# A graph layer's node stage: six slots of x for four, and GpSimd loads two of the six

## What is computed

```python
h = relu(layernorm(x))
msg = relu(h[src] + edge_attr)
p = msg @ W_fc.T + b_fc                         # one row of 256 for each edge
w = exp(p @ Q.T - segment_max(p @ Q.T, dst)[dst])       # four heads
alpha = w / max(segment_sum(w, dst)[dst], 1e-9)
pooled[:, h] = segment_sum(alpha[:, h] * p, dst)        # for each head
gate = softmax((segment_sum(p, dst) / max(deg, 1)) @ Wg.T + bg)
out = x + sigmoid(sum_h gate[:, h] * pooled[:, h])      # one row of 256 for each node
```

## Time and profile before

| | |
|---|---|
| median of three executions | 657.8 us (657.22 to 658.36) |
| the profiled execution | 653.4 us, span of the profile 651.3 us |
| granted TensorE clock, mean | 0.968 |
| busy share of the span: TensorE, VectorE, ScalarE, GpSimd | 83%, 71%, 64%, 70% |
| DMA | 171.54 MB, mean 263 GB/s |
| chain that ended last, largest lines | TensorE L803 22%, TensorE L895 22%, L788 5%, ScalarE L649 4%, GpSimd L516 4% |
| first sigmoid of the node stage | at 327.94 us |

### The profile page before, as it was taken

How to read it: one execution, slowest core, us unless ns; L and a number is a source line. 1 busy time by engine, 2 the same in 40 slices (tenths; PEclk the granted TensorE clock), 3 DMA queues, 4 the chain that set the end, 5 groups by cost and what they waited for, 6 DMA issues and landing times.

```text
span 651.3 us, 12707 instructions
## 1 busy us (share of the span) xinstructions
PE 543.0 (83%) x2670; PEld 439.9 (68%) x2671; DVE 462.0 (71%) x1607; ACT 416.3 (64%) x765; POOL 454.9 (70%) x342
## 2 busy tenths in 40 slices
PE   2799999999999999920899989878878876878775
PEld 2588888888887778810687768666666665656554
DVE  3986878998999998779776667555646555456454
ACT  1667778888897888723035556656665665666674
POOL 6777777777777777107045677787887878778784
PEclk9998999999999999975799999999999999899999
DMA  8566666766668899530289999999999999999999
GB/s 206 165 198 166 201 194 211 219 203 204 197 189 284 295 300 315 181 129 1 72 285 350 386 345 320 320 331 351 312 318 326 354 314 334 318 304 348 327 342 324
DMA packets 137275, 171.54 MB, mean 263 GB/s; under 512 B 10132, under 2 KB 123820, under 8 KB 137238
## 3 DMA queue, kind: packets, MB, share of 16 engines
q10 hardware_dynamic: 91344, 90.23, 42.3%
q1 hardware_dynamic: 33046, 42.70, 20.6%
q0 software_dynamic: 12848, 38.20, 18.5%
HBM read 111.50 MB, written 59.60 MB: 263 GB/s over the span
## 4 chain that ended last, share of the span: by engine, by line
PE 54%; DVE 15%; ACT 9%; issue 8%; POOL 4%; ACTq 3%; DVEq 3%; DMA 3%; POOLq 0%; SPq 0%
PE bank L803 22%; PE bank L895 22%; PE bank L788 5%; ACT arena L649 4%; POOL arena L516 4%; DVE spread L1406 4%; ACT bank L625 3%; PE bank L800 3%; DVE stats L1214 2%; ACTq L652 2%; DVEq L1410 1%; DMA p_keep<-in_x_dram,idx 1%; DVE arena L1220 1%; DVEq L1406 1%; DMA arena<-in_x_dram 1%
## 5 line engine op out<-in xcount | busy, mean ns | idle before, releaser
L895 PE MATMUL bank<-p_keep,spread 128*128 x1172 | 274.5, 388 | 54.3 <-DVE spread L1406 43.4
L895 PEld LDWEIGHTS bank<-p_keep,spread 128*128 128x128 f32 x1172 | 218.7, 192 | 110.9 <-issue 83.7
L1406 DVE TENSOR_SCALAR spread<-bank,rel,wgt 128x128 f32<-128x128 f32 x586 | 195.6, 403 | 131.4 <-PE bank L895 82.2
L516 POOL TENSOR_TENSOR arena<-arena 128x1024 f32<-128x1024 f32 x96 | 224.9, 2353 | 74.9 <-ACT arena L649 74.3
L803 PE MATMUL bank<-w_all,arena 128*128 128x264 f32 (+1 forms) x784 | 208.8, 389 | 0.0
L649 ACT ACTIVATE arena<-bank 128x1024 f32<-128x1024 f32 x97 | 99.3, 1023 | 139.7 <-PE bank L895 130.7
L479 POOL DMA_INDIRECT p_keep<-in_x_dram,idx x124 | 124.5, 1004 | 38.8 <-issue 31.4
L803 PEld LDWEIGHTS bank<-w_all,arena 128*128 128x128 f32 (+1 forms) x784 | 135.3, 192 | 15.8
L625 ACT ACTIVATE bank<-zero 128x1024 f32<-128x1024 f32 x98 | 100.5, 1026 | 3.0
L543 ACT ACTIVATE arena<-bank 128x256 f32<-128x256 f32 x196 | 74.2, 379 | 33.2 <-PE bank L788 32.6
L479 POOL DMA_INDIRECT arena<-in_x_dram,idx x72 | 73.5, 1020 | 23.1 <-issue 14.9
(11 more groups left out here) (248 smaller groups left out, 239.5 us busy)
## 6 DMA issues: line engine op xcount, KB each, us to landing
out_dram<-arena ACTq DMA_DIRECT2D x97, 512.0 KB, 4.4
arena<-in_x_dram ACTq DMA_DIRECT2D x73, 512.0 KB, 5.3
arena<-in_edge_attr_dram SPq DMA_DIRECT2D x48, 512.0 KB
arena<-in_x_dram POOLq DMA_DIRECT2D x24, 512.0 KB, 5.6
p_spill<-p_keep SPq DMA_DIRECT2D x16, 512.0 KB, 3.9
p_keep<-p_spill SPq DMA_DIRECT2D x16, 512.0 KB, 5.0
p_keep<-in_x_dram,idx POOLq DMA_INDIRECT x124, 2.8
arena<-in_x_dram,idx POOLq DMA_INDIRECT x72, 5.0
```

What stands on the lines that cost most here:

```text
L516: pool.tensor_tensor(yout[:, slot, :, :], yout[:, slot, :, :], xin[:, slot, :, :], ALU.add).then_inc(summed, 1)
L895: nc.tensor.matmul(places[:, bass.ds(place, T)], spread[:, k0 + k, :], p_rows[:, bass.ds(p_at, T)], start=False, stop=True, skip_group_che ...
L1406: v.tensor_scalar(spread[:, k, :], bank[:, 7, P:2 * P], rel[:, bass.ds(s0 + k, 1)], wgt[:, bass.ds(s0 + k, 1)], ALU.is_equal, ALU.mult).th ...
```

## The change

`xin` becomes a list of six slots of four tiles: the four of before and two more in the floats 8192 to 10239 of the arena (eight KB), where the early softmax had its tiles. ScalarE loads groups 0 to 3 as early as before, and groups 4 and 5 once the second matmul of the table of weights is done (`wgt_summed` at 2). In the loops ScalarE now loads x for group g+5, into the slot that the add of g-1 has freed. GpSimd issues the loads of slots 0 and 3 of the six, each for six groups later, which is after every third group; before, it was slot 0 of four, after every fourth. GpSimd issues 32 loads rather than 24. Its loop is written out for the first and the last twelve groups and rolled in twelves between (`add_twelve`). The last two, smaller, loads of x are issued in the iteration of group 92 rather than 94. Nothing else differs: the adds, the stores, the sigmoids, the steps and the PSUM slots are the same.

```diff
--- before.py
+++ after.py
@@ -97,11 +97,12 @@
     FULL = N // (GROUP * P)
     assert GROUPS == FULL + 1 and FULL % 2 == 1
     LAST_WHOLE = (N - FULL * GROUP * P) // P
-    XS, YS = 4, 4
+    XS, YS = 6, 4
+    XS_EARLY = 4
     PERIOD = 12
     ROUNDS = FULL // PERIOD
-    BY_POOL = (0,)
-    assert FULL % 4 == 1 and (FULL - 1) % 4 in BY_POOL
+    BY_POOL = (0, 3)
+    assert (FULL - 1) % PERIOD == 0 and (FULL - 1) % XS in BY_POOL and PERIOD % YS == 0
     assert PERIOD % SLOTS == 0 and PERIOD % XS == 0 and LAST_WHOLE == 2 and N % P and FULL % PERIOD == 1
 
     scratch = nc.dram_tensor("p_spill", [SPILL // 4 * P, 4 * T], F32).ap()
@@ -160,7 +161,7 @@
         o = 0
         xg = arena[:, o:o + BODY * D].rearrange("p (t d) -> p t d", d=D); o += BODY * D
         u = arena[:, o:o + 4 * D].rearrange("p (t d) -> p t d", d=D); o += 4 * D
-        assert o >= XS * GROUP * D
+        assert o >= XS_EARLY * GROUP * D
         ea = arena[:, o:o + BODY * D].rearrange("p (t d) -> p t d", d=D); o += BODY * D
         msg_t = arena[:, o:o + 4 * D].rearrange("p (t c e) -> p t c e", c=KD, e=P); o += 4 * D
 
@@ -172,7 +173,7 @@
 
         wa, a1, a2, a3 = (heads(o + k * HE) for k in range(4)); o += 4 * HE
         assert o <= 10240
-        o = XS * GROUP * D
+        o = XS_EARLY * GROUP * D
         wb, top, gate, run, tot, mean, prod = (heads(o + k * HE) for k in range(7)); o += 7 * HE
         total_a, total_b = a3[:, 2, :], prod[:, 2, :]
 
@@ -195,7 +196,7 @@
         mx, o = small(arena, o, BLK, 2)
         last_a, o = small(arena, o, P)
         last_b, o = small(arena, o, P)
-        assert o <= (XS + YS) * GROUP * D, o
+        assert o <= (XS_EARLY + YS) * GROUP * D, o
         after_rows = logits[:, :, :].rearrange("p t k -> p (t k)")
         sel_1 = after_rows[:, 0:BLK * STEPS].rearrange("p (b s) -> p b s", b=BLK)
         chain = after_rows[0:C, 0:2 * (TILES + 1)].rearrange("p (s t) -> p s t", s=2)
@@ -229,8 +230,11 @@
 
         pair = lambda a: a.rearrange("p (g k) e -> p g k e", g=2)
 
-        xin = arena[:, 0:XS * GROUP * D].rearrange("p (s q d) -> p s q d", s=XS, q=GROUP)
-        yout = arena[:, XS * GROUP * D:(XS + YS) * GROUP * D].rearrange("p (s q d) -> p s q d", s=YS, q=GROUP)
+        def four_tiles(k):
+            return arena[:, k * GROUP * D:(k + 1) * GROUP * D].rearrange("p (q d) -> p q d", q=GROUP)
+
+        xin = [four_tiles(k) for k in (0, 1, 2, 3, 8, 9)]
+        yout = arena[:, XS_EARLY * GROUP * D:(XS_EARLY + YS) * GROUP * D].rearrange("p (s q d) -> p s q d", s=YS, q=GROUP)
 
         tail = p_keep[:, RING - TAIL:RING, :].rearrange("p t d -> p (t d)")
         o = 0
@@ -506,24 +510,25 @@
 
             x_later = x[0:FULL * GROUP * P, :].rearrange("(t p) d -> p t d", p=P)
 
-            def add_four(g0, first, more):
-                for slot in range(4):
-                    pool.wait_ge(sig_done, g0 + slot + 1)
-                    if first or slot not in BY_POOL:
-                        pool.wait_ge(x_in[slot], g0 * 4 + 16)
+            def add_twelve(g0, round_, first, last):
+                for k in range(PERIOD):
+                    g, slot = g0 + k, k % XS
+                    pool.wait_ge(sig_done, g + 1)
+                    if slot not in BY_POOL:
+                        pool.wait_ge(x_in[slot], round_ * (16 * PERIOD // XS) + 16 * (k // XS) + 16)
+                    elif first and k < XS:
+                        pool.wait_ge(x_in[slot], 16)
                     else:
-                        pool.wait_ge(x_pool[slot], g0 * 4)
-                    pool.tensor_tensor(yout[:, slot, :, :], yout[:, slot, :, :], xin[:, slot, :, :],
-                                       ALU.add).then_inc(summed, 1)
-                    if slot in more:
-                        pool.wait_ge(summed, g0 + slot + 1)
-                        pool.dma_start(xin[:, slot, :, :], x_later[:, bass.ds((g0 + slot + XS) * GROUP, GROUP), :]
-                                       ).then_inc(x_pool[slot], 16)
-
-            add_four(0, True, BY_POOL)
-            with pool.Fori(1, FULL // 4 - 1) as four:
-                add_four(four * 4, False, BY_POOL)
-            add_four(FULL - FULL % 4 - 4, False, [k for k in BY_POOL if FULL - FULL % 4 + k < FULL])
+                        pool.wait_ge(x_pool[slot], round_ * (16 * PERIOD // XS) + 16 * (k // XS))
+                    pool.tensor_tensor(yout[:, k % YS, :, :], yout[:, k % YS, :, :], xin[slot], ALU.add).then_inc(summed, 1)
+                    if slot in BY_POOL and (not last or k + XS <= PERIOD):
+                        pool.wait_ge(summed, g + 1)
+                        pool.dma_start(xin[slot], x_later[:, bass.ds((g + XS) * GROUP, GROUP), :]).then_inc(x_pool[slot], 16)
+
+            add_twelve(0, 0, True, False)
+            with pool.Fori(1, FULL // PERIOD - 1) as twelve:
+                add_twelve(twelve * PERIOD, twelve, False, False)
+            add_twelve(FULL - 1 - PERIOD, FULL // PERIOD - 1, False, True)
 
         @block.scalar
         def _(act):
@@ -600,10 +605,10 @@
             x_rows = x[0:FULL * GROUP * P, :].rearrange("(t p) d -> p t d", p=P)
 
             def load_x(g, slot):
-                act.dma_start(xin[:, slot, :, :], x_rows[:, bass.ds(g * GROUP, GROUP), :]).then_inc(x_in[slot], 16)
+                act.dma_start(xin[slot], x_rows[:, bass.ds(g * GROUP, GROUP), :]).then_inc(x_in[slot], 16)
 
             act.wait_ge(ln_done, TILES)
-            for g in range(XS):
+            for g in range(XS_EARLY):
                 load_x(g, g)
 
             act.wait_ge(keep_turned, 1)
@@ -631,15 +636,18 @@
                 clear(z)
             act.wait_ge(words_in, 64)
             act.wait_ge(wgt_ready, 1)
+            act.wait_ge(wgt_summed, 2)
+            for g in range(XS_EARLY, XS):
+                load_x(g, g)
             o_rows = out[0:FULL * GROUP * P, :].rearrange("(t p) d -> p t d", p=P)
             last_row = (FULL * GROUP + LAST_WHOLE) * P
 
             def load_last_x():
                 slot = FULL % XS
-                act.dma_start(xin[:, slot, 0:LAST_WHOLE, :],
+                act.dma_start(xin[slot][:, 0:LAST_WHOLE, :],
                               x[FULL * GROUP * P:last_row, :].rearrange("(t p) d -> p t d", p=P)
                               ).then_inc(x_in[slot], 16)
-                act.dma_start(xin[0:N % P, slot, LAST_WHOLE, :], x[last_row:N, :]).then_inc(x_in[slot], 16)
+                act.dma_start(xin[slot][0:N % P, LAST_WHOLE, :], x[last_row:N, :]).then_inc(x_in[slot], 16)
 
             def places(z, n):
                 return bank[:, 2 * z:2 * z + 2, :].rearrange("p b (h t) -> p (b h) t", h=2)[:, 0:n, :]
@@ -671,8 +679,8 @@
                 clear(k % SLOTS)
                 if k:
                     store(k - 1, (k - 1) % YS)
-                if k + 3 >= XS and (k + 3) % XS not in BY_POOL:
-                    load_x(k + 3, (k + 3) % XS)
+                if k and (k + XS - 1) % XS not in BY_POOL:
+                    load_x(k + XS - 1, (k + XS - 1) % XS)
             with act.Fori(1, ROUNDS - 1) as r:
                 for k in range(PERIOD):
                     g = r * PERIOD + k
@@ -683,8 +691,8 @@
                     act.wait_ge(sig_done, g + 1)
                     clear(k % SLOTS)
                     store(g - 1, (k - 1) % YS)
-                    if (k + 3) % XS not in BY_POOL:
-                        load_x(g + 3, (k + 3) % XS)
+                    if (k + XS - 1) % XS not in BY_POOL:
+                        load_x(g + XS - 1, (k + XS - 1) % XS)
             for g in range((ROUNDS - 1) * PERIOD, FULL):
                 if g % 3 == 0:
                     steps = steps_of(g // 3)
@@ -694,9 +702,9 @@
                     act.wait_ge(sig_done, g + 1)
                     clear(g % SLOTS)
                 store(g - 1, (g - 1) % YS)
-                if g + 3 < FULL and (g + 3) % XS not in BY_POOL:
-                    load_x(g + 3, (g + 3) % XS)
-                elif g + 3 == FULL:
+                if g + XS - 1 < FULL and (g + XS - 1) % XS not in BY_POOL:
+                    load_x(g + XS - 1, (g + XS - 1) % XS)
+                elif g + XS - 1 == FULL:
                     load_last_x()
             slot = FULL % YS
             act.wait_ge(stored[slot], 16 * (FULL // YS))
@@ -1438,17 +1446,17 @@
             dve.wait_ge(zeroed, GROUPS)
             spreads(s0, HALF, STEPS - s0 - HALF)
 
-            slot = (FULL - 1) % 4
+            slot, x_slot = (FULL - 1) % YS, (FULL - 1) % XS
             dve.wait_ge(sig_done, FULL)
-            dve.wait_ge(x_pool[slot], 16 * ((FULL - 1) // 4))
-            v.tensor_tensor(yout[:, slot, :, :], yout[:, slot, :, :], xin[:, slot, :, :], ALU.add).then_inc(last_summed, 1)
-            slot, left = FULL % 4, N % P
+            dve.wait_ge(x_pool[x_slot], 16 * ((FULL - 1) // XS))
+            v.tensor_tensor(yout[:, slot, :, :], yout[:, slot, :, :], xin[x_slot], ALU.add).then_inc(last_summed, 1)
+            slot, x_slot, left = FULL % YS, FULL % XS, N % P
```

(6 more changed lines are left out.)

## The result

Six executions of each kernel on one chip: 663.36 us (660.26 to 667.45) for the changed one, 656.71 (654.93 to 658.36) for the one before, ratio 1.0099 with a 95% interval of 1.0059 to 1.0139. On a second chip, with the kernel before beside it, the ratio was 1.0146 (1.0095 to 1.0196). The profiled execution of the changed kernel took 667.5 us, the slowest of its six, so its terms are read against 653.4 with that in mind.

The account below looks back on a forecast made before the run. Bound: a ring of spread, matmul, sigmoid and clear through three PSUM slots, plus a chain through ScalarE's and GpSimd's queues. Only the loop term, +6.7 us, was nonzero: 653.4 to 660.1, plus 4.4 carried over gave 664.5; range 658 to 671.

Parts of the forecast that it names:

- my high end: Rolled loop, groups 12 to 83: long three-group rounds stay, short ones are lifted to their minimum times, adding 8.5 us.
- Transfers and depth: 0: Node stage: loading five groups ahead rather than three removes no wait, since no add waits for x; 0 us.
- The rival of 631 us: Node stage: transfers set the pace, so more in flight lift 324 to 367 GB/s, 27 us less; chance 0.03.
- the chain in every three: Rolled loop: a delay through GpSimd's and ScalarE's queues would recur every three groups, not six of 24 times; +6.7 us, chance 0.71.
- the word: ScalarE's read of step counts ahead of every third sigmoid, claimed as one condition for the costly two-queue chain.
- threes: Rounds of three groups, between starts of every third sigmoid; 24 in the rolled loop, 9.67 us each before the change.
- the sign that I gave: Changed profile's loop: every third sigmoid 9.8 us or more after the one three before, none at 8.
- the floor of 9.76: Rolled loop: predicted minimum for three groups, except the first of each twelve (9.84 us) and the last (10.11).
- held-back store: ScalarE's store of group 3j+1, waiting for an add that GpSimd's load of x after add 3j delays.
- The floors: Rolled loop: minimum times of three-group rounds, 39.47 us per twelve groups, 236.8 us in all, +4.8 us.
- that wait among the rivals: GpSimd's idle 2.7 us ahead of one load; rival that its delays add up, 14 us, so 672; chance 0.09.
- The margin that the prediction named as a way to be wrong: Node stage: time could go instead to stores that land later than a sigmoid of four groups on; no size given.

Follow-up runs that it names:

- six slots alone: Changed kernel with GpSimd's loads of x back after every fourth group (0, 4, 8 of twelve): ratio 1.0001 to the kernel before, 654.65 us against 653.79.
- the pattern alone: Changed kernel with four slots of x instead of six, GpSimd's loads still after every third group: ratios 1.0193 and 1.0214 to the kernel before.
- moving the word out of the chain: Changed kernel, ScalarE's step-count read moved ahead of the store in three of four three-group rounds: ratio 0.9992 to the kernel before.
- two groups later: Changed kernel with GpSimd's loads after groups 2, 5, 8, 11 of twelve: ratio 1.0003 to the kernel before.
- no load on GpSimd: Changed kernel with ScalarE issuing all loads of x in the node stage, one behind each store: ratio 0.9971 to the kernel before.
- load ahead of the store: Changed kernel with ScalarE's load issued ahead of the store and its wait, four groups ahead rather than five: ratio 1.0162 to the kernel before.
- the shift by one: Changed kernel with GpSimd's loads after groups 1, 4, 7, 10 of twelve: ratio 0.9894 to the kernel before (647.38 us), again 0.9893.

## Why the prediction was right

**The direction and the size.** Forecast +6.7 us; measured 663.36 - 656.71 = 6.65 us, and 0.0146 x 654.5 = 9.6 us on the second chip. The predicted 664.5 us lies 1.1 above the median. That the first difference agrees to 0.05 us is luck. In both profiles of the changed kernel the loop is longer by more than the 8.5 us of my high end: by 10.1 and, with 243.0 us, by 11.1. The profiled execution of the kernel before (653.4 us) was faster than all six timed ones and the changed kernel's first profile is its slowest of six, so part of these 10 to 11 us is the spread of executions; how much the loop costs in a median execution stays open. The 4.4 us that I carried over from the profile to the median is 656.71 - 653.4 = 3.3 with all six executions of the kernel before.

**Transfers and depth: 0.** Shown by six slots alone (1.0001). The rival of 631 us is out: at a DMA share of 0.98 the loop of the changed kernel waits for no load to land. The Trainium skill (page "Perfetto Trace Analysis", section "What 'DMA-bound' means") lists the 16 DMA engines among the things that a kernel can be bound on. Judged by their busy share this stage looked like that case; the depth experiment decides against it here.

**GpSimd's loads: the chain in every three.** That it is the pattern is shown three ways: the pattern alone brings the loss, the same number of loads one group later turns it into a gain, and moving the word out of the chain takes it away. The threes of the changed loop average 242.1 / 24 = 10.09 us (9.67 before). None is near 8, but the sign that I gave, 9.8 us or more, holds for 14 of the 24 only, and three are under 9.5 (9.02, 9.41, 9.44), which the floor of 9.76 forbids. There the word was read faster, in 0.29 us in the shortest; the floor was built with its usual 0.87 us, and in the kernel before it took 0.29 to 1.28.

**Where three things meet.** I had said that the chain costs only where a held-back store, a load and the word meet. The runs say that two parts cost by themselves. What stands ahead of sigmoid 3j is a held-back store and, apart from it, a load with the word behind it. Read the placements so: both present 1.010 and 1.015 (changed kernel); only load and word 1.000 (two groups later) and 0.997 (no load on GpSimd); neither 0.989. Only the held-back store, with the word moved away, gives 0.999, though there one three in four still has both. So each part costs about 1%, the held-back store perhaps less, and the second the kernel before was already paying in three of four threes. I had priced it at nothing. Moving the word in the kernel before, which this reading says should gain, was not run.

**The term that was missing.** The floors give 236.8 us for the loop and the forecast had 238.7; the profile has 242.1, 5.3 above the floors. Five threes are together 6.8 us above them, and the other 19 together 1.6 below. The longest of the five, from sigmoid 15 to 18, took 11.83 us. In it GpSimd waits 2.71 us rather than 0.68 ahead of its load, and the store and the sigmoid behind it come later by that:

```profile
396.61 0.77 POOL L526 DMA_DIRECT2D arena<-in_x_dram  x1 [2.71 <-issue]
```

The floor of 9.76 with 2.03 more is 11.79, and this three lasted 11.83 to 11.85 in all four profiles of the changed kernel and of the pattern with four slots. I had named that wait among the rivals ("2.7 us long", "once in 18") and left it out of the sum. It comes once in the kernel before too, but ahead of the load after group 20, where the chain doesn't close; in the changed kernel it falls on the load after group 15, where it does.

The other four (those that start at sigmoids 33, 54, 63 and 69, of 11.19, 11.17, 10.71 and 11.44 us) hold a stretch at half clock. The first and the last of them, each with the stretch ahead of it, and the one of the kernel before:

```profile
449.00:456.50 7.50, 4.64 (x21) 3.46 (x20) 2.31 (x8) 4.10 (x4) 5.73 (x4) 1.00 0.98 314
456.50:459.90 3.40, 3.40 (x9) 2.50 (x9) 1.76 (x6) 1.34 (x2) 2.62 (x2) 0.50 1.02 351
...
569.20:575.90 6.70, 2.88 (x13) 2.23 (x13) 1.43 (x5) 3.62 (x5) 5.46 (x3) 1.00 0.97 321
575.90:579.30 3.40, 3.40 (x8) 2.77 (x9) 2.78 (x9) 0.82 (x1) 2.83 (x2) 0.51 1.01 309
```

```profile
564.80:568.20 3.40, 3.40 (x9) 2.72 (x9) 2.00 (x6) 0.95 (x1) 1.24 (x1) 0.50 1.07 382
```

TensorE was idle for 2.9 of the 7.5 us ahead of the first and 3.8 of the 6.7 ahead of the last, then ran 3.4 us at 1.2 GHz rather than 2.4. Each costs at most 1.7 us of matmul time. These four threes are 1.0 to 1.4 us above their floors. In the loop the five profiles of kernels that are 1% or more slower than the one before (changed, four slots with the pattern, load ahead of the store) have four to six such stretches, those of all others none to three (the kernel before one; the shift by one, one and none). That longer waits bring the half clock, and so are paid twice, fits this count; no experiment separates the two.

**Small slips.** GpSimd issues 31 loads, not 32, since the load after group 93 has no group of its own, and ScalarE issues 7 fewer. Ahead of the loop, where I had 0, the profile has 1.6 us more, and it has 0.6 more from sigmoid 84 to 96.

**"Nothing waits for a landing."** True of the body of the loop, not of its edge: where the rolled loop begins, sigmoids 11 and 13 wait 1.3 and 0.63 us for a store. The margin that the prediction named as a way to be wrong is the one that the load ahead of the store fell into.

## What to carry to other kernels

Before adding work to a queue, look for a chain that leaves through one queue and returns through another, and see where its period and the period of the added work meet; here 30 or 31 issues cost 1.0% to 1.5% or gained 1% by where they stood. A distance that recurs to the hundredth of a microsecond (9.83, four times) pointed to such a chain, and it could be priced from the trace before anything was built. Taking the chain apart by moving one piece at a time showed what the price hid: that two of its parts cost by themselves. A busy share of 0.98 to 1.00 on the DMA engines says nothing on its own: ask who waits for a landing, and test depth alone.

## What the runs showed of the hardware

With stores issued right behind loads on the same queue, their median landing was after 6.4 us, against 4.3 us in the kernel where the store went first. ScalarE's read of one word from SBUF took 0.29 us in most cases of the shift by one, where no load stood close ahead of it, and 0.5 to 1.4 us in most others; in the experiment with the load ahead of the store it was long without a load close by, so what sets it stays open. GpSimd's sixth load of x waited 2.71 or 2.72 us rather than 0.68 in all 13 profiles of kernels in which it issues such loads, whether that load stood behind group 15, 16, 17 or 20; nothing that the profile shows ended the wait, and why it is the sixth stays open.
